# A state-space scan stage in a six-stage decoder: the next batch's preparation and the last batch's gate placed inside a batch's scan

## The reference, cut to what matters

```python
# layer 1, x: [4, 512, 512], 16 heads of 32
q, k, v = x @ q_w.T + q_b, x @ k_w.T + k_b, x @ v_w.T + v_b      # by heads
qp, kp = elu(q) + 1, elu(k) + 1
kv = einsum('bhsd,bhse->bhde', kp, v)
z  = einsum('bhsd,bhd->bhs', qp, kp.sum(axis=2))
x1 = layernorm(x + (qp @ kv / (z + 1e-6)) @ o_w.T + o_b)
# layer 2, hidden = ctx [4, 512, 256], 512 channels, 16 states
u  = silu(causal_conv4(ctx @ in_proj_w.T) + conv_b)
dt_low, B, C = split(u @ x_proj_w.T, [16, 32])
dt = softplus(dt_low @ dt_proj_w.T + dt_b)
state = exp(dt * A) * state + (dt * u) * B        # for each of 512 places
y  = (state * C).sum(states) + D * u
x2 = layernorm(x1 + y * silu(x1))
```

## Time and profile before

| | |
|---|---|
| median of the runs | 2951.9 us |
| profiled execution: its own time | 2950.78 us |
| profiled execution: span | 2948.8 us |
| mean granted TensorE clock, share of full | 0.95 |
| busy over the span: PE, DVE, ACT, POOL | 2639.7, 2067.5, 1178.3, 641.9 us |
| first stage, from the start to the first VectorE operation of the next | 866.3 us |
| first scan operation of batches 0, 1 and 3 | at 79.25, 285.46 and 705.21 us |

### The profile page before, as it was taken

One profiled execution on the slowest core, in us unless ns is written; L12 is line 12 of the kernel. 1 busy time (PEld: TensorE's weight loads), 2 busy tenths in 40 slices (PEclk: granted clock), 3 DMA queues, 4 the chain that ended last, 5 costly groups with the idle time before them and its releaser, 6 DMA issues.

```text
span 2948.8 us, 30680 instructions
## 1 busy us (share of the span) xinstructions
PE 2639.7 (90%) x9586; PEld 1640.0 (56%) x9586; DVE 2067.5 (70%) x4063; ACT 1178.3 (40%) x2139; POOL 641.9 (22%) x569
## 2 busy tenths in 40 slices
PE   6888888888869978789989999999989998999998
PEld 2333333333337844456657666666666665488886
DVE  3996996996996547778876888588867887322232
ACT  4335325326333312255554555355544555121111
POOL 0642543534520135411101111011101110000000
PEclk9998988988979999999999999999999999999999
DMA  3111111111220212233233222332222223400000
GB/s 120 57 50 44 65 43 55 61 50 51 69 109 29 79 43 86 77 122 101 86 102 116 83 83 76 92 108 83 83 74 95 83 72 107 138 1 29 29 15 14
DMA packets 90792, 212.58 MB, mean 72 GB/s; under 512 B 9987, under 2 KB 34819, under 8 KB 86534
## 3 DMA queue, kind: packets, MB, share of 16 engines
q1 hardware_dynamic: 81510, 178.51, 18.7%
q0 software_dynamic: 5472, 21.01, 1.9%
q10 hardware_dynamic: 3648, 11.08, 1.0%
HBM read 164.10 MB, written 46.47 MB: 71 GB/s over the span
## 4 chain that ended last, share of the span: by engine, by line
PE 59%; DVE 20%; issue 11%; POOL 5%; ACT 3%; DMA 1%; SPq 1%; DVEq 0%; POOLq 0%; ACTq 0%
PE bank L594 21%; PE bank L844 8%; PE bank L912 3%; DVE h L1441 3%; PE bank L984 3%; PE bank L985 3%; PE bank L988 3%; POOL h L1822 3%; DVE val L1640 2%; DVE sm L1734 2%; DVE val L1648 2%; PE bank L714 2%; PE bank L970 2%; PE bank L960 2%; PE bank L961 1%
## 5 line engine op out<-in xcount | busy, mean ns | idle before, releaser
L1822 POOL TENSOR_TENSOR h<-du,Bb 128x1024 f32<-128x1024 f32 x128 | 306.2, 2394 | 188.1 <-DVE h L1446 172.2
L1441 DVE TENSOR_TENSOR_SCAN h<-bank,h 128x512 f32<-128x512 f32 x256 | 297.8, 1203 | 22.4 <-POOL h L1822 15.1
L1095 ACT ACTIVATE bank<-dt,A 128x512 f32<-128x512 f32 x256 | 175.9, 691 | 327.7 <-DVE h L1441 327.6
L1240 ACT ACTIVATE p<-bank,sm,rq 128x512 f32<-128x512 f32 x256 | 199.1, 778 | 244.5 <-DVE sm L1738 244.5
L1890 POOL TENSOR_TENSOR rq<-rq,mhalf 128x4 f32<-128x4 f32 x64 | 69.4, 1084 | 798.3 <-DVE rq L1692 798.3
L594 PE MATMUL bank<-pT,v 128*128 128x512 f32 x512 | 236.7, 606 | 2.7 <-ACT pT L1040 2.7
L211 POOL TENSOR_SCALAR rstd<-mv 128x1 f32<-128x1 f32 x96 | 25.2, 263 | 956.5 <-DVE mv L205 956.5
L594 PE MATMUL bank<-kr,q 128*128 128x512 f32 x512 | 233.0, 598 | 0.0
L714 PE MATMUL bank<-h,ident 128*128 128x512 f32 x256 | 153.2, 682 | 84.6 <-DVE h L1446 84.5
L844 PE MATMUL bank<-x_hi,wxq_s 128*128 128x512 f32 x512 | 190.8, 454 | 6.5 <-DVE x_lo L1713 6.5
L1648 DVE COPY_PREDICATED val<-msk,val 128x258 f32<-128x258 int32 x448 | 173.6, 449 | 27.8 <-DVE val L1648 0.2
(11 more groups left out here) (228 smaller groups left out, 5686.4 us busy)
## 6 DMA issues: line engine op xcount, KB each, us to landing
wxq_s<-wq_dram SPq DMA_DIRECT2D x48, 512.0 KB, 4.5
Bb<-bc_dram SPq DMA_DIRECT2D x32, 512.0 KB, 3.6
Cb<-bc_dram SPq DMA_DIRECT2D x32, 512.0 KB, 3.7
x_dram<-xo POOLq DMA_DIRECT2D x16, 1024.0 KB, 4.7
xc<-x_dram SPq DMA_DIRECT2D x16, 1024.0 KB, 5.2
woh<-in_Wo SPq DMA_DIRECT2D x64, 256.0 KB, 2.7
wxv_s<-wkv_dram SPq DMA_DIRECT2D x12, 1024.0 KB, 5.3
wxk_s<-wkv_dram SPq DMA_DIRECT2D x12, 1024.0 KB, 7.4
```

The costliest lines, as they stand in the source:

```text
L1095: act.activation(bank[2 + n][:, :], dt[:, et, :], ACT.Exp, scale=A[:, et, 2 * w + n:2 * w + n + 1]).then_inc(dA_ready, 1)
L1240: act.activation(p4[:, t, :], bank[4 + t][:, :], ACT.Exp, bias=sm4[:, 4 + t:5 + t], scale=rq[:, hh % 2, 1, t:t + 1], accum_out=sm4[:, 8 + ...
L1441: dve.tensor_tensor_scan(h[:, s, n, :], bank[2 + n][:, :], h[:, s, n, :], 0.0, ALU.mult, ALU.add).then_inc(scanned, 1)
L1822: pool.tensor_tensor(h[:, U % HR, :, :], du[:, et:et + 1, :].to_broadcast([P, 2, S]), Bb[:, w % 2, :, :], ALU.mult).then_inc(dBu_ready, 1)
```

## The change

All of it is in the first stage.

- The loop over the batches is written out, and two of the three parts above move. The preparation of batch c + 1 (context products, convolution, `u`, `xdbl`, `dt`, softplus) stands between the units of batch c's scan. The end of batch c (gate, turning back, norms) stands between units 0 to 3 of batch c + 1. The turning of the next x stands at units 30 and 31. The query products of batch c stand at its own units 13 to 16. Batch 0's preparation is still ahead of everything, and batch 3's end behind everything.
- All products but the y pair share banks 0 and 1 in one written list `USES`; each use waits until the use two before it was read.
- The convolution reads the product in PSUM itself, and `xpad` and its copies are gone. D u is four TensorE products with a diagonal matrix that open the sums in banks 4 to 7 (L801). Softplus works on pairs of tiles: relu, abs, exp, 1 + exp on ScalarE, one VectorE operation for the rounding rest, one Ln over all four tiles, one subtraction, one addition. It doesn't use the ring `h` or `du` any more; `dt` has two buffers.
- A bias is one product of the type fp32r: a 6-row `pick` by 6 rows that hold each bias as a rounded part and a rest.
- The normaliser z is computed as 64 columns on 128 partitions (16 products of 16 columns, four transposes) in place of 512 columns on 16 partitions.
- `bc_dram` is written from ScalarE's queue. On SyncE's queue the load of x for batch c + 1 stands ahead of the first B and C of batch c, and from batch 1 on it waits for the last output product of batch c - 1 to be read.

```diff
-            with pe.Fori(0, B // 2) as i:
-                for p in range(2):
-                    c = 2 * i + p
...
+            for c in range(B):
+                more = c + 1 < B
+                for U in range(NU):
+                    if U in (0, 1) and c:
+                        turn_gated(c - 1, 2 * U)
+                        turn_gated(c - 1, 2 * U + 1)
+                    if U == 0:
+                        pe.wait_ge(u_ready, START + after(c, KI, KI))
+                        for et in range(KI):
+                            pe.wait_ge(y_gated, START + after(c - 1, KI, et + 1) if c else START)
+                            pe.matmul(bank[4 + et][:, :], diagD[:, et, :], u[:, et, :], start=True, stop=False)
+                    if U in range(3, 7):
+                        keys(c, U - 3)
+                    if U in (7, 12) and more:
+                        et = (U - 7) // 5 * 2
+                        in_project(c + 1, et)
+                        in_project(c + 1, et + 1)
+                    if U in range(8, 12):
+                        values(c, U - 8)
+                    if U in range(13, 17) and c:
+                        queries(c, U - 13)
+                    if U == 17 and more:
+                        in_xdbl(c + 1)
+                    if U == 18:
+                        keys_values(c)
...
+            def use(*name):
+                k = USES[name]
+                for last, n in USES.items():
+                    if n == k - 2:
+                        pe.wait_ge(*FREED[last])
+                return bank[k % 2]
...
+            def conv(c, et):
+                d, free = full("in", c, et)
+                dve.wait_ge(du_ready, START + after(c, KI, 0))
+                dve.tensor_scalar(u[:, et, :], d[:, :], cw[:, et, KW - 1:KW], None, ALU.mult).then_inc(conv_step, 1)
...
+                    if U == 0 and c:
+                        gated(c - 1)
...
+                    if U in (7, 12) and more:
+                        et = (U - 7) // 5 * 2
+                        conv(c + 1, et)
+                        conv(c + 1, et + 1)
+                    if U in range(15, 19) and c:
+                        query(c, U - 15)
...
+                    if U == 25 and more:
+                        minus_rest(c + 1, 0)
+                        minus_rest(c + 1, 1)
+                    if U == 27 and more:
+                        logs_rest(c + 1)
+                    if U == 28 and more:
+                        add_relu(c + 1)
...
+                if c + 1 < B:
+                    sp.wait_ge(*FREED["in", c, KI - 2])
+                    sp.wait_ge(*FREED["in", c, KI - 1])
+                    load_ctx0(c + 1)
+                    if c:
+                        sp.wait_ge(ln_sum, START + after(c - 1, 8, 4))
+                    load_x(c + 1, (c + 1) % 2, x_in)
```

More of the change, by code:

```diff
@@ L228, in build @@
         qb = s1("qb", [P, KD]); qbn = s1("qbn", [P, KD])
-        rows = s1("rows", [1, 3, D])
+        rows = s1("rows", [6, D], F32R); pick = s1("pick", [6, 3, P], F32R); parts = s1("parts", [6, 4])
+        diagD = s1("diagD", [P, KI, P])
         cw = s1("cw", [P, KI, KW]); cb = s1("cb", [P, KI])
@@ L725, in _ @@
+            for t in range(NT):
+                turn_gated(B - 1, t)
             if stages >= 2:
@@ new lines, in query, with key, gate_u @@
+            def query(c, n):
+                exp_relu(8 * c + n + (4 if c else 0), ("q", c, n), qb[:, n:n + 1], qbn[:, n:n + 1])
+            def key(c, t):
+                if c and t == 0:
+                    act.wait_ge(*FREED["at", c - 1, 2])
+                    act.wait_ge(*FREED["at", c - 1, 3])
+                exp_relu(8 * c + t + (0 if c else 4), ("k", c, t), 0.0, 0.0)
+            def gate_u(c):
+                for et in range(KI):
+                    act.wait_ge(*FREED["in", c, et])
+                    act.activation(u[:, et, :], u[:, et, :], ACT.Silu, bias=cb[:, et:et + 1]).then_inc(u_ready, 1)
@@ L1113, in _ @@
+            gate_x1(B - 1)
             if stages >= 2:
@@ L1492, in _ @@
+            gated(B - 1)
+            first_gated(B - 1, 0)
+            for t in range(1, NT):
+                first_gated(B - 1, t)
+                last_gated(B - 1, t - 1)
+            last_gated(B - 1, NT - 1)
             if stages >= 2:
@@ L1836, in scores_of @@
+            for t in range(2, 8):
+                ln_pool(pool, after(B - 1, 8, t), t % 2)
+            store_chunk(0, B - 1)
             def scores_of(c, b):
```

745 lines of the change are left out of this document (449 added, 296 removed).

## The result

The changed kernel takes 2925.3 us (median of 4 runs, 2924.2 to 2928.7) against 2952.1; the ratio is 0.9915, 95% interval 0.9898 to 0.9932. The profiled execution took 2924.2 us, its span is 2922.5. The forecast was 2916, so the sign and the mechanism came out, and the gain is 27 us instead of 36.

A forecast was written before the change was run, and what follows sets the result against it. VectorE sets the pace in the scan, a chain from engine to engine between scans. Start, four batches and end sum to 830 against 866.3 for the first stage, 36 us gained: 2916 us, range 2855 to 2953.

The forecast's parts named there:

- Start, 84.5: First scan of batch 0 begins at 84.5 us in place of 79.25, bounds 76 and 90.
- U0 to U3, 31: First four units of a middle batch, with the last batch's gate and norms: 31 us, bounds 25 and 35.
- U4 to z, 92: Units U4 to U19 of a middle batch: TensorE, with 88 us, later than VectorE's 74.5; 92 with hand-overs and stall.
- U20 to the next scan, 72.4: Rest of a middle batch: 65.6 us for U20 to U31, 0.8 for the normaliser, 6 for the boundary.
- The boundary term of 6: At each of the first two batch boundaries B waits behind the load of x: 6 us; the third costs 1.
- Batch 2, 190.4: Length of batch 2: 190.4 us, against 195.4 for batch 1; its boundary has no x load and costs 1.
- Batch 0, 178.7: Length of batch 0, without gate or queries; VectorE's work and waits, rest of the scan and boundary: 178.7 us.
- Batch 3, 165.3, and the end, 16: Batch 3, with no preparation to hide, takes 165.3 us; its end takes 16 of the earlier 19.3.
- The table switch: Silu behind U14 with two table loads at 1.28 us stalls about 1.9; 2.66 a switch would make 2924.
- Rival A: VectorE alone decides, the ring of six slots taking up TensorE's lag: gain of 157 us, 2795; chance 0.17.
- Rival B: TensorE's granted clock at 0.85 of full in U4 to U19: 15.5 us a batch more, 2978, slower; chance 0.12.
- Rival C: No change: GpSimd and SyncE order costs 14 us more at boundaries, batch 0's start 8 more; chance 0.13.

The follow-up runs named there:

- short queries: Changed kernel with the query products of batches 1 to 3 made from one of their four pieces on TensorE; 2922.2 us.
- B first: Changed kernel with the first window's B and C issued on SyncE ahead of the next batch's context and x; 2915.3 us.
- convolutions later: Changed kernel with VectorE's convolutions behind a scan's 9th and 15th unit instead of 8th and 13th, Silu of u one unit later; 2909.5 us.
- both edits: Changed kernel with B and C issued ahead of the next batch's context and x, and VectorE's convolutions one and two units later; 2899.0 us.
- One tap: Changed kernel with only the first of the convolution's four taps kept in batches 1 to 3, 9 us a batch less VectorE work; 2912.3 us.

## Why the prediction was right in kind and 9 us too hopeful

The stage was forecast 13.5 us too short (830.3 against 843.8); the parts missed by 1.5, 6.7, 3.0, 5.7, -3.8 and 0.4 us. That the time is only 9 us off is luck: what follows the stage, forecast as unchanged, happened to take 3.8 us less.

- **Start, 84.5.** 86.0; within its bounds.
- **U0 to U3, 31.** 300.68 - 271.44 = 29.2. Right, with the pause of TensorE in it that I had put at 1 us late: it was 11.23, beside VectorE's work and so free there, but not free behind it.
- **U4 to z, 92.** 395.82 - 300.68 = 95.1, against VectorE's 74.0 us of its own (74.5 forecast): the lag of TensorE came back as VectorE's waits, as forecast, 18.1 us for TensorE where 15 to 20 was the test. The size: seven biases at 0.43 and not 0.25, 1.3 us; the first y pair and key product at the low clock, 3.0; the hand-overs, of which I charged 4, 5.2 for the two of h alone. The convolution's first tap took 0.75 and not 0.5. And the words "TensorE, with 88, is the later one", said of all of U4 to U19, were too wide: the short queries show that behind the third convolution VectorE does.
- **U20 to the next scan, 72.4 with the normaliser and the boundary.** 469.81 - 395.82 = 74.0. The boundary term of 6 was VectorE's 4.76 and 1.9 for the longer norm operation; B first measured it at 7 to 8 with what the clock added. The mechanism (B behind the load of x) is shown by that run. GpSimd could start 265.75 - 259.77 = 6.0 us after B's issue, between B alone (3.6) and what the forecast took from the transfer issued behind x (7.8), and the 6 taken was right. The Trainium skill, "DMA: Bandwidth & Descriptors", section "Queues, rings and completion order", says that on each SDMA engine descriptors are consumed in ring order. The trace agrees: x landed at 264.41 and B at 265.68, 1.3 us behind the whole of it. What was too high was the 8 us drawn from it, as x itself landed in 5.1 us here.
- **Batch 2, 190.4.** 196.1, the largest miss of a middle batch, with no boundary wait of its own. With B first, which shortens the pause of 11 us at its start, it is 190.6, and with 11 products in that pause it is 190.6 too. So the 5.5 us are what the pause did to the clock and, through it, to VectorE's waits. The forecast had no term for it; it had put TensorE's lateness in U0 to U3 at 1 us and its clock there at nothing.
- **Batch 0, 178.7.** 185.4, the largest miss: 7.07 and 7.93 us ahead of the convolutions where I put 6.4 and 5.8 (the terms given for the 6.4 make 6.7), and 6.7 for a boundary of 6. That is 3.5 of the 6.7; about 2 more are this execution's, as the same batch took 183.3 in three others. With convolutions later it is 177.6, with both edits 167.7.
- **Batch 3, 165.3, and the end, 16.** 161.5 and 16.4; 3.8 on the good side.
- **The table switch.** Silu behind U14 cost VectorE 1.84 us, 1.9 forecast. The page's 2.66 us for each switch (the Trainium skill, "ScalarE: Activation LUTs", "What ACT_TABLE_LOAD costs") would have given 2924. That is near the time by chance: in the trace the loads stay at 1.28 us, and Silu starts 0.02 us behind its load (363.26 and 364.56).
- **Rival A** (VectorE alone, 2795) did not come; its waits for TensorE are there in every batch. One tap shows that VectorE's time still counts almost whole; what A had wrong is that TensorE's counts beside it.
- **Rival B** (clock) came in part. I had set 0.95 in the chain's stretch as the line between my forecast and B: it was 0.94 there, a hair on B's side. Over whole batches it was 0.90, 0.91, 0.89 and 0.95, and 0.93, 0.90, 0.91 and 0.94 before, so the clock as a whole hardly fell. It didn't turn the sign, as it came in spells of 3 to 14 us, most of them beside other waits, and not as 0.85 throughout. In the experiments B's mechanism is there too: spells of 10 to 17 us, each of which cost VectorE 3 to 7 us.
- **Rival C** had the right place for part of the loss, the boundary, at half its price or less: it has 14 us more than the 6 charged for each of two, and B first gave back 20 for both.

What the forecast did not ask is which part pays. Hiding the preparation gains 44 us of the stage, hiding the gate about 12; the kernel without the first is 21 slower than before, 13 of which are the later first h at the batch starts. What of the rest is D u, the new softplus or the gate inside the scan was not separated. The biases are not the reason: a bias took 0.43 us in place of 1.05.

## What to carry to other kernels

When two nearly full engines hand buffers to each other in order, find the pairs of waits that mirror one another (5.17 on one side, 2.47 on the other just behind it) and move the consumer's step one turn later; that gained 22 us of a stage without taking work from any engine. In such a pair the time of either engine counts, however the busy shares look: 27 us taken from the one and 21 from the other came back as 18 each, the first with a spell of low clock in it. When a producer is then moved earlier, move the consumer that frees its buffer with it: done alone it made batch 0 8.5 us longer, and moving the consumer too took 6 to 10 us off each of three batches. And before hiding work in a loop, look at the queue behind it at the loop's edge: one load ahead of the transfer that the next batch starts with cost 20 us in a stage where the whole change had gained 22 (by the times, 10 of 27). And when one batch of an experiment contradicts the others, read its clock first: one tap and both reorderings each look 7 to 11 us smaller than they are.

## What the runs showed of the hardware that was not expected

- The granted clock fell to 0.50 for 10 to 17 us while TensorE ran without a pause (e.g. 1.00 over 360 to 370, 0.50 over 376 to 390 with TensorE busy in all of it), behind the normaliser's 16-column products and among 16-row ones. It is at that place in five of the twelve experiments, and the same code had it in some batches and not in others: in the changed kernel's batch 1 the clock at that place was low from 396 to 399 only, and 1.00 over 400 to 417. What decides it is open.
- A pause ahead of a product often costs a second time: D u took 5.66 us behind a pause of 11.23, 4.29 behind one of 4.45 and 3.60 behind busy products.
- A bias of 6 rows in the one-pass format costs 0.43 us for 512 columns, one instruction, where the float32 one of 1 row cost 1.05 in two.
- The norm's operation on VectorE takes 2.48 us in place of 0.54 when GpSimd's 1024-wide product runs beside it (269.04 and GpSimd's row from 268.90; 0.53 at 288.70, where GpSimd is idle), which made each late `rstd` 1.9 us dearer.
